# Bucket numbers of four (six) chunks packed into one word, taken apart in VectorE's registers

## The chip, the cores and the metric

The kernel runs on one core of a Trainium2 chip. The metric is the device time of one execution in microseconds (us); most executions of this kernel agree within 0.1%. The engines are TensorE (PE, with its weight loads as PEld), VectorE (DVE), ScalarE (ACT), GpSimd (POOL) and SyncE (SP). Each has a sequencer of its own that issues its instructions; in the trace the sequencer's own work (register operations, loads of registers, waits) stands under the engine's name with a q (DVEq). SBUF is the on-chip memory of 128 partitions, PSUM the memory that TensorE writes.

## The reference

Four layers over a graph with 3125 nodes of 256 features and 50000 edges: a weighted edge sum, a mixture of four experts whose gates come from a graph attention on a second graph of 32768 edges, three graph attention layers on the first graph, and a routed feed-forward layer. Cut to what the change touches:

```python
x = x + segment_sum(edge_weight[:, None] * (layernorm(x) @ W)[dst], src, 3125) + bias   # 50000 edges
def _gat_conv(x, src, dst, W, a_src, a_dst, b, n_nodes):     # once with 4 heads of 4, three times with 4 heads of 64
    h = (x @ W).reshape(n_nodes, Hh, Cc)
    e = leaky_relu(e_src[src] + e_dst[dst], 0.2)
    m = segment_max(e, dst)
    ex = exp(e - m[dst])
    denom = segment_sum(ex, dst)
    out = segment_sum(h[src] * (ex / (denom[dst] + 1e-16))[:, :, None], dst)
    return out.reshape(n_nodes, Hh * Cc) + b
```

## The kernel before, in words

The program is a row of stages, each ended by a barrier of all engines. Within a stage every engine has its own instruction list, written in the order in which it runs, and counts semaphores to wait for the others; there is no scheduler.

**The sort.** The edges of each graph are sorted by the node that they are summed into, on the chip. `place_edges` (for the edge sum) puts them into buckets of 128 nodes, `place_fine` (for the two attention graphs) into buckets of 32 nodes, 100 in all. A bucket starts at a new chunk, a column of 128 edges, so every chunk belongs to one bucket; the edge sum has 415 chunks, the attention graphs up to 360 and 504. Which bucket a chunk belongs to is found with a matrix product, and VectorE copies the numbers from PSUM into the integer tile `bucket` (L234, L359), one column a chunk, the same value in every partition. In the same stage as `place_fine` GpSimd scatters the edges of the first sort (`scatter_edges`), and VectorE goes on with `permute_edges`.

**The edge sum** (`sum_edges`). Loop over 415 chunks, unrolled. GpSimd gathers 128 rows by an indirect DMA (L651, 16 buffers), VectorE makes a 128x128 one-hot matrix (`mark`, L625), TensorE multiplies (L662, 8 banks of PSUM), VectorE adds the product to row `b` of the accumulator `acc` (`take`, L631). `b`, the bucket's number, must be in a register of VectorE's sequencer, since it enters the address. Every fourth chunk four numbers are loaded (L640). An addition waits for the product (`summed`) and for the addition before it (`taken`).

**The attention** (`attend_edges`), once 16 wide (stage from 1860 us) and three times 256 wide (from 2942, 3819 and 4693 us). Its unit is a quad of QD = 4 chunks; a loop body has U = 6 quads, a first and a last body are unrolled. For a quad q:

- GpSimd gathers four times 128 rows (L709), 6 quads ahead; before it, it waits that TensorE has used the buffer (`summed`, L707).
- VectorE prepares the scores of q + 1 (`fence`, L728), TensorE turns them (L870), VectorE reduces those of q to maxima (L757, waits for `turned`), ScalarE adds a bias (L821), VectorE carries the running maximum on (L763, L769, L774, L778) and applies the leaky slope (`leak`, L748), ScalarE takes exponentials (L831), TensorE turns back (L878), ScalarE copies (L838), TensorE forms the four sums (L886).
- VectorE adds the sums of quad q - 2 to `acc` (`add_up`, L743, four times: t = 0 to 3), each between two steps of the running maximum. The buckets' numbers come from `load_buckets` (L732), which loads four words into registers and stands after L728 and ahead of the reduction. Each addition waits for the one before it (`taken`).

After the last body the additions of the last two quads follow without other work between.

Of the kernel before, what the change touches and what calls it, by code (L numbers as in the profile page):

```python
# [10 lines left out]
NT = (N + P - 1) // P  # L11
# [6 lines left out]
HEADS = 4  # L18
QD = 4
GROUP = 24  # L20
DB = 32
STEP = 2.0 ** 50
NS = 4 * NT
LN_EPS = 1e-5
BIG = 1e30

ALU = mybir.AluOpType
# [8 lines left out]
NCS = (E + NT * (P - 1)) // P  # L36


def columns_sorted(edges):

    worst = (edges + -(-N // DB) * (P - 1)) // P
    return -(-worst // GROUP) * GROUP

# [87 lines left out]
    return 400 if edges == E else 256  # L131


def place_edges(nc, block, m, name, key_in, val_in, w_in, rec_dram, record, row, bucket):


# [21 lines left out]
    past, ps_bucket = m.work[0:NT, 0:ncol], m.psum[2][:, 0:ncol]  # L158
# [21 lines left out]
    def _(dve):  # L180
        chain = Chain(dve, steps)
# [50 lines left out]

        dve.wait_ge(counted, 1)
        chain.next(nc.vector.tensor_copy(bucket, ps_bucket))  # L234


def place_fine(nc, block, m, name, key_in, val_in, nch, record, bucket, own_hot, starts, trip_count):
# [23 lines left out]
    ps_bucket, ps_start = m.psum[2][:, 0:nch], m.psum[3][:, 0:nch]  # L261
# [21 lines left out]
    def _(dve):  # L283
        chain = Chain(dve, steps)
# [6 lines left out]
        dve.wait_ge(loaded, 32)  # L291
        nc.vector.tensor_scalar(lo_i, key, DB - 1, None, ALU.bitwise_and)
        nc.vector.tensor_scalar(valid, key, float(NT * P), None, ALU.is_lt)
        chain.next(nc.vector.tensor_scalar(place, key, 5, None, ALU.logical_shift_right))
        chain.next(nc.vector.tensor_copy(hi, place))
        for g in range(4):
            at = slice(g * NB, (g + 1) * NB)
# [24 lines left out]
            n = NB  # L322
# [31 lines left out]
        last = cend[:, NS - 1:NS]  # L354
        chain.next(nc.vector.tensor_scalar(hi[:, 0:nch // GROUP], m.iotac[:, 0:nch // GROUP], float(GROUP), last, ALU.mult, ALU.is_lt))
        chain.next(nc.vector.tensor_reduce(total[:, 0:1], hi[:, 0:nch // GROUP], AX.X, ALU.add))
        chain.next(nc.vector.tensor_scalar(trip_count, total[:, 0:1], -2.0, None, ALU.add))
        dve.wait_ge(summed, 1)
        nc.vector.tensor_copy(bucket, ps_bucket)  # L359
        chain.next(nc.vector.tensor_scalar(starts, ps_start, -BIG, None, ALU.mult))  # L360

def permute_edges(nc, block, m, name, edges, nch, record, lows, rows):

# [246 lines left out]
def sum_edges(nc, block, m, name, table, rec, index, bucket):  # L610


    hot, summed, taken, cleared = (m.sem(f"{name}_{s}") for s in ("hot", "summed", "taken", "cleared"))
    f = m.sums
    RS, PS = len(f.rows), len(f.hot)
    landed = [m.dma_sem(f"{name}_landed{s}") for s in range(RS)]
    ps = [m.psum[s][:, 0:D] for s in range(PS)]
    part = rec.rearrange("p (c k) -> p c k", k=3)

    @block.vector  # L620
    def _(dve):
        def mark(c):
            if c >= PS:
                dve.wait_ge(summed, c - PS + 1)
            nc.vector.tensor_scalar(f.hot[c % PS][:, :], m.iota[:, :], part[:, c, 0:1], part[:, c, 2:3], ALU.is_equal, ALU.mult).then_inc(hot, 1)  # L625

        def take(c, b):
            dve.wait_ge(summed, c + 1)
            if c:
                dve.wait_ge(taken, c)  # L630
            nc.vector.tensor_tensor(m.acc[:, b, 0:D], m.acc[:, b, 0:D], ps[c % PS], ALU.add).then_inc(taken, 1)  # L631

        nc.vector.memset(m.acc[:, :, :], 0.0).then_inc(cleared, 1)
        dve.wait_ge(cleared, 1)
        for c in range(PS):
            mark(c)
        for c in range(NCS):
            if c % 4 == 0:
                n = min(4, NCS - c)
                b = nc.values_load_multi_w_load_instructions(bucket[0:1, c:c + n], [mybir.EngineType.DVE], min_val=0, max_val=NT,  # L640
                                                             skip_runtime_bounds_check_because="a bucket's number counts up to 25 buckets")[1]
            take(c, b[c % 4])
            if c + PS < NCS:
                mark(c + PS)

    @block.gpsimd
    def _(pool):
        for c in range(NCS):
            if c >= RS:
                pool.wait_ge(summed, c - RS + 1)  # L650
            nc.gpsimd.indirect_dma_start(  # L651
                out=f.rows[c % RS][:, :], out_offset=None, in_=table,
                in_offset=bass.IndirectOffsetOnAxis(ap=index[:, c:c + 1], axis=0)).then_inc(landed[c % RS], 16)

    @block.tensor
    def _(pe):
        for c in range(NCS):
            pe.wait_ge(hot, c + 1)
            if c >= PS:
                pe.wait_ge(taken, c - PS + 1)  # L660
            pe.wait_ge(landed[c % RS], 16 * (c // RS + 1))
            nc.tensor.matmul(ps[c % PS], f.hot[c % PS][:, :], f.rows[c % RS][:, :], start=True, stop=True).then_inc(summed, 1)  # L662


def attend_edges(nc, block, m, name, width, table, at_dram, nch, lows, rows_in, bucket, own_hot, starts, trip_count):
# [6 lines left out]
    rw = hw + HEADS  # L672
    U = GROUP // QD
    s_ = lambda n: m.sem(f"{name}_{n}")
# [5 lines left out]
    rows = [f.rows[s][:, :, 0:rw] for s in range(U)]  # L680
# [9 lines left out]
    edges = E if nch == NCF else EG  # L690
    least, most = -(-edges // (P * GROUP)) - 2, nch // GROUP - 2

    @block.sync
    def _(sp):
        sp.dma_start(f.at[0:NS, :, :], at_dram.rearrange("q (s d) -> s q d", d=DB)).then_inc(at_in, 16)
        for h in range(HEADS):
            sp.dma_start(acc[DB * h:DB * (h + 1), :, :], table[:, h * w1:(h + 1) * w1].rearrange("(s d) c -> d s c", d=DB)).then_inc(acc_in, 16)
        sp.wait_ge(acc_in, 16 * HEADS)
# [22 lines left out]
    def _(dve):  # L721
        def fence(q, s, turn):
# [3 lines left out]
            if not isinstance(q, int) or q >= 2:  # L726
                dve.wait_ge(turned, q + (-1))
            nc.vector.tensor_tensor(f.z[s % 2], rows[s][:, :, hw:rw].unsqueeze(3).to_broadcast([P, QD, HEADS, DB]),  # L728
                                    f.pen[s % 2][:, :, :].unsqueeze(2).to_broadcast([P, QD, HEADS, DB]), ALU.subtract).then_inc(masked, 1)

        def load_buckets(q):
            return nc.values_load_multi_w_load_instructions(bucket[0:1, bass.ds(q * QD, QD)], [mybir.EngineType.DVE], min_val=0, max_val=NS - 1,  # L732
                                                            skip_runtime_bounds_check_because="a bucket's number is a sum of one-hot rows times 0 to 99")[1]

        def add_up(q, s, t, b):
            if t == 0:
# [61 lines left out]
        for k in range(2):  # L798
            q = trips * U + (2 * U - 2 + k)
            b = load_buckets(q)  # L800
            for t in range(QD):
                add_up(q, U - 2 + k, t, b[t])
# [528 lines left out]
def memory(nc, ctx):  # L1331
# [70 lines left out]
    def view(*shape):  # L1402
        n = 1
        for d in shape:
            n *= d
        v = m.work[:, at[0]:at[0] + n]
        at[0] += n
        if len(shape) == 2:
            v = v.rearrange("p (a b) -> p a b", a=shape[0])
        if len(shape) == 3:  # L1410
            v = v.rearrange("p (a b c) -> p a b c", a=shape[0], b=shape[1])
        return v
# [6 lines left out]
    f = m.flash = Memory()  # L1419
    slots = GROUP // QD  # L1420
    f.rows = [view(QD, D + 2 * HEADS) for _ in range(slots)]
# [153 lines left out]
```

## Time and profile before

| | us |
|---|---|
| median of 3 runs | 5848.58 (5844.78 to 5849.41) |
| the profiled execution | 5906.44 |
| its span | 5904.7 |
| VectorE busy | 3167.8 (54%) |
| TensorE busy, matmuls | 3100.8 (53%) |
| GpSimd busy | 2848.6 (48%) |
| ScalarE busy | 1892.7 (32%) |

The page has the busy time of each engine in 40 slices of the span, the DMA queues, and groups of instructions: line, engine, operation, names of what is written and read, shape and count, then busy time and the mean of one in ns, then the idle time of the engine just before them with what ended it. "remote" is a releaser that the trace doesn't name; "issue" is time in which the engine waited for nothing that the trace shows. Of no engine is the busy share over 54%, so the ends of waits tell more than busy times. From 1860 us on the four attention layers take up most of the time; TensorE's granted clock is 0.50 in them, 1.2 GHz.

### The profile page before, as it was taken

How to read it: one execution, taken by the hardware profiler on the slowest of the kernel's cores; microseconds unless marked ns; L12 is line 12 of the kernel's file. 1: busy time of each engine (PE TensorE's matmuls, PEld its weight loads, DVE VectorE, ACT ScalarE, POOL GpSimd, SP SyncE). 2: the span in 40 equal slices, each digit the busy share in tenths (PEclk: the TensorE clock that was granted, in tenths of full speed). 3: DMA queues.
4: the chain of work that ended last, by engine and by line, in shares of the span. 5: the costliest groups of instructions: out<-in, count | busy, mean ns of one | idle time of the engine just before them, and what ended most of it. 6: DMA issues, size and time to landing. Idle time of an engine off the chain costs nothing. (4 is left out here: it accounts for less than half of the span.)

```text
span 5904.7 us, 84687 instructions
## 1 busy us (share of the span) xinstructions
PE 3100.8 (53%) x22441; PEld 1829.3 (31%) x22441; DVE 3167.8 (54%) x8455; ACT 1892.7 (32%) x6583; POOL 2848.6 (48%) x2704
## 2 busy tenths in 40 slices
PE   0234048575735444899555555455555455555194
PEld 0111011132323222566333333333333333333163
DVE  7799999644462445111445555455555455555614
ACT  0000000000003555111155555365556256555210
POOL 2877887266643664000166665166655266655100
PEclk9678579756565555999755555655555655555597
DMA  1000000233321000000233333333333333333000
GB/s 62 25 1 4 0 1 2 70 92 91 92 61 10 8 7 6 22 7 0 64 85 80 81 80 79 74 81 80 81 81 74 81 81 80 80 80 69 16 0 24
DMA packets 200623, 297.12 MB, mean 50 GB/s; under 512 B 110599, under 2 KB 139750, under 8 KB 200454
## 3 DMA queue, kind: packets, MB, share of 16 engines
q0 software_dynamic: 108656, 245.98, 16.6%
q1 hardware_dynamic: 91830, 49.55, 3.3%
q8 instruction: 57, 0.93, 0.1%
q14 instruction: 80, 0.66, 0.0%
HBM read 272.32 MB, written 23.05 MB: 50 GB/s over the span
## 5 line engine op out<-in xcount | busy, mean ns | idle before, releaser
L709 POOL DMA_INDIRECT work<-table_att,work x1368 | 1385.5, 1013 | 1725.0 <-ACT work L807 834.5
L886 PE MATMUL psum<-work 128*32 128x65 f32 (+1 forms) x13248 | 418.2, 295 | 984.9 <-ACT work L838 974.1
L757 DVE TENSOR_REDUCE work<-psum 128x512 f32 (+1 forms) x414 | 286.0, 691 | 1164.2 <-remote 1162.0
L418 POOL DMA_INDIRECT sorted<-stage_rec,stage_row x400 | 676.7, 1692 | 177.0 <-issue 126.2
L878 PE MATMUL psum<-ident,work 128*128 128x128 f32 x1656 | 559.4, 474 | 379.2 <-ACT work L831 295.4
L886 PEld LDWEIGHTS psum<-work 128*32 128x32 f32 x13248 | 331.0, 165 | 1104.9 <-issue 1018.2
L831 ACT ACTIVATE work<-work 128x128 f32<-128x128 f32 x1656 | 529.9, 391 | 133.8 <-issue 100.3
L493 ACT ACTIVATE stats<-stats 128x25 f32<-128x25 f32 x5 | 1.1, 223 | 1697.0 <-DVE stats L483 1697.0
L651 POOL DMA_INDIRECT work<-table_sum,index x415 | 396.9, 956 | 290.2 <-SPq L1473 92.6
L838 ACT COPY work<-psum 128x512 f32<-128x512 f32 x414 | 242.7, 586 | 885.4 <-remote 829.5
L821 ACT ACTIVATE work<-psum,work 128x128 f32<-128x128 f32 x1656 | 473.7, 369 | 146.3 <-DVE work L757 97.5
L878 PEld LDWEIGHTS psum<-ident,work 128*128 128x128 f32 x1656 | 301.2, 182 | 681.9 <-ACT work L831 430.5
L662 PE MATMUL psum<-work 128*128 128x256 f32 x830 | 377.0, 584 | 251.9 <-DVE work L625 135.3
L743 DVE SCALAR_TENSOR_TENSOR acc<-acc,work,psum 128x65 f32 (+1 forms) x1656 | 445.3, 269 | 75.7 <-issue 13.3
L870 PE MATMUL psum<-ident,work 128*128 128x128 f32 x1656 | 462.0, 435 | 37.7 <-DVE work L728 26.0
L709 POOL DMA_INDIRECT work<-table_gate,work x288 | 294.7, 1023 | 310.3 <-ACT work L807 129.7
L397 PE MATMUL psum<-work 128*128 128x504 f16 (+1 forms) x1312 | 364.9, 362 | 97.7 <-DVE work L381 40.9
L814 ACT ACTIVATE work<-iota,lows 128x32 f32<-128x32 f32 x1656 | 401.8, 332 | 1.7 <-issue 1.7
L631 DVE TENSOR_TENSOR acc<-acc,psum 128x256 f32 x415 | 174.9, 421 | 320.8 <-PE psum L662 163.1
L870 PEld LDWEIGHTS psum<-ident,work 128*128 128x128 f32 x1656 | 296.3, 217 | 103.7 <-issue 71.2
L662 PEld LDWEIGHTS psum<-work 128*128 128x128 f32 x830 | 193.3, 270 | 435.7 <-DVE work L625 239.8
L728 DVE TENSOR_TENSOR work<-work 128x512 f32<-128x512 f32 x414 | 284.8, 688 | 62.5 <-DMA work<-table_att,work 29.6
(300 smaller groups left out, 4600.0 us busy)
## 6 DMA issues: line engine op xcount, KB each, us to landing
work<-table_att,work POOLq DMA_INDIRECT x1368
table_att<-acc SPq DMA_DIRECT2D x75, 132.0 KB
acc<-table_att SPq DMA_DIRECT2D x12, 812.5 KB
work<-table_sum,index POOLq DMA_INDIRECT x415
sorted<-stage_rec,stage_row POOLq DMA_INDIRECT x400
sorted<-work SPq DMA_DIRECT2D x8, 622.5 KB, 7.9
work<-sorted SPq DMA_DIRECT2D x8, 622.5 KB
work<-table_gate,work POOLq DMA_INDIRECT x288
```

The costliest lines, as they stand in the source:

```text
L397: ins = nc.tensor.matmul(ps[k], row_hot[s][:, k, :], col_hot[s], start=f == 0, stop=f == fc - 1)
L418: nc.gpsimd.indirect_dma_start(out=rec_dram[s * half + f], out_offset=bass.IndirectOffsetOnAxis(ap=m.stage_row[s][:, f:f + 1], axis=0), in ...
L651: nc.gpsimd.indirect_dma_start(out=f.rows[c % RS][:, :], out_offset=None, in_=table, in_offset=bass.IndirectOffsetOnAxis(ap=index[:, c:c + ...
L662: nc.tensor.matmul(ps[c % PS], f.hot[c % PS][:, :], f.rows[c % RS][:, :], start=True, stop=True).then_inc(summed, 1)
L709: nc.gpsimd.indirect_dma_start(out=rows[s][:, t, :], out_offset=None, in_=table[:, 0:rw], in_offset=bass.IndirectOffsetOnAxis(ap=f.index[s ...
L743: nc.vector.scalar_tensor_tensor(acc[:, b, :], acc[:, b, :], f.fac[s][:, t:t + 1], ps_s[s % 2][:, t, :], ALU.mult, ALU.add).then_inc(taken, 1)
L814: ins = nc.scalar.activation(f.pen[s % 2][:, t, :], m.iota[:, 0:DB], ACT.Square, scale=STEP, bias=lows[:, bass.ds(q * QD + t, 1)])
L821: ins = nc.scalar.activation(f.y[s % 2][:, t, :], ps_z[s % 2][:, t * P:(t + 1) * P], ACT.Identity, bias=dst[:, bass.ds(q * QD + t, 1)])
L831: nc.scalar.activation(f.pt[s % 2][:, t, :], f.y[s % 2][:, t, :], ACT.Exp, bias=f.neg[s][:, t, 1:2]).then_inc(exped, 1)
L870: ins = nc.tensor.transpose(ps_z[s % 2][:, t * P:(t + 1) * P], f.z[s % 2][:, t, :, :].rearrange("p h d -> p (h d)"), m.ident[:, :])
L878: nc.tensor.transpose(ps_p[s % 2][:, t * P:(t + 1) * P], f.pt[s % 2][:, t, :], m.ident[:, :]).then_inc(turned2, 1)
L886: ins = nc.tensor.matmul(ps_s[s % 2][DB * h:DB * (h + 1), t, :], f.p[s % 2][:, t, DB * h:DB * (h + 1)], rows[s][:, t, h * w1:(h + 1) * w1] ...
```

## The change

The numbers of several chunks are put into one integer where `bucket` is made: in `place_edges` six numbers of 5 bits (PACK0 = 6), in `place_fine` four numbers of 7 bits (QD). Column k of each group is overwritten by (column k + 1 shifted left) or (column k), from the last but one down to the first, so the first column of a group ends with all of them. That is five small operations in the first sort and three in each of the other two. In `place_fine` the copies into `starts` and `bucket` change places. `load_word` loads the one word of a group, and `unpack` makes a number of it with register operations (shift, then mask). `sum_edges` loads a word every six chunks, `load_buckets` one word a quad.

```diff
+PACK0 = 6
...
+def packs(bucket, k):
+    n = bucket.shape[1] // k
+    return bucket[:, 0:n * k].rearrange("p (q t) -> p q t", t=k)
+
+
+def load_word(dve, nc, at):
+    return nc.values_load_multi_w_load_instructions(at, [mybir.EngineType.DVE], min_val=0, max_val=2 ** 30 - 1,
+                                                    skip_runtime_bounds_check_because="bit fields of at most 30 bits")[1][0]
+
+
+def unpack(nc, dve, word, bits, t, most):
+    return nc.s_assert_within((word >> (bits * t)) & (2 ** bits - 1), 0, most, skip_runtime_bounds_check_because="packed from numbers of buckets in this range")
...
         chain.next(nc.vector.tensor_copy(bucket, ps_bucket))
+        packed = packs(bucket, PACK0)
+        for k in reversed(range(PACK0 - 1)):
+            chain.next(nc.vector.scalar_tensor_tensor(packed[:, :, k], packed[:, :, k + 1], 5, packed[:, :, k], ALU.logical_shift_left, ALU.bitwise_or))
...
         dve.wait_ge(summed, 1)
-        nc.vector.tensor_copy(bucket, ps_bucket)
-        chain.next(nc.vector.tensor_scalar(starts, ps_start, -BIG, None, ALU.mult))
+        nc.vector.tensor_scalar(starts, ps_start, -BIG, None, ALU.mult)
+        chain.next(nc.vector.tensor_copy(bucket, ps_bucket))
+        packed = packs(bucket, QD)
+        for k in reversed(range(QD - 1)):
+            chain.next(nc.vector.scalar_tensor_tensor(packed[:, :, k], packed[:, :, k + 1], 7, packed[:, :, k], ALU.logical_shift_left, ALU.bitwise_or))
...
-            if c % 4 == 0:
-                n = min(4, NCS - c)
-                b = nc.values_load_multi_w_load_instructions(bucket[0:1, c:c + n], [mybir.EngineType.DVE], min_val=0, max_val=NT,
-                                                             skip_runtime_bounds_check_because="a bucket's number counts up to 25 buckets")[1]
-            take(c, b[c % 4])
+            if c % PACK0 == 0:
+                word = load_word(dve, nc, bucket[0:1, c:c + 1])
+            take(c, unpack(nc, dve, word, 5, c % PACK0, NT))
...
         def load_buckets(q):
-            return nc.values_load_multi_w_load_instructions(bucket[0:1, bass.ds(q * QD, QD)], [mybir.EngineType.DVE], min_val=0, max_val=NS - 1,
-                                                            skip_runtime_bounds_check_because="a bucket's number is a sum of one-hot rows times 0 to 99")[1]
+            word = load_word(dve, nc, bucket[0:1, bass.ds(q * QD, 1)])
+            return [unpack(nc, dve, word, 7, t, NS - 1) for t in range(QD)]
```

The register operations of `unpack` are emitted where the number is used, behind the waits of the addition. On VectorE, in the loop of a 256 wide layer, before, from the load of a quad's numbers on (ISA is an address computation of the sequencer, REGISTER_ALU one register operation):

```order
L732 ISA
L732 TENSOR_LOAD bucket2
L757 ISA
L757 TENSOR_REDUCE work<-psum 128x4
L743 ISA
L743 SCALAR_TENSOR_TENSOR acc<-acc,work,psum 128x65
L763 ISA x2
L763 SCALAR_TENSOR_TENSOR work<-work 128x8
L742 REGISTER_ALU
L743 ISA
L743 SCALAR_TENSOR_TENSOR acc<-acc,work,psum 128x65
```

The same place of the changed kernel (its lines are 9 to 19 higher; L141 is `load_word`):

```order
L141 ISA
L141 TENSOR_LOAD bucket2
L776 ISA
L776 TENSOR_REDUCE work<-psum 128x4
L762 REGISTER_ALU
L762 ISA
L762 SCALAR_TENSOR_TENSOR acc<-acc,work,psum 128x65
L782 ISA x2
L782 SCALAR_TENSOR_TENSOR work<-work 128x8
L761 REGISTER_ALU
L762 REGISTER_ALU x2
L762 ISA
```

The order of engine instructions is the same; ahead of the first addition of a quad stands one more register operation, ahead of each of the other three stand two more.

On VectorE in the edge sum, before, from a load on:

```order
L640 TENSOR_LOAD bucket0
L631 ISA
L631 TENSOR_TENSOR acc<-acc,psum 128x256
L625 TENSOR_SCALAR work<-iota,rec 128x128
L631 ISA
```

and of the changed kernel:

```order
L141 TENSOR_LOAD bucket0
L652 REGISTER_ALU
L652 ISA
L652 TENSOR_TENSOR acc<-acc,psum 128x256
L646 TENSOR_SCALAR work<-iota,rec 128x128
L652 REGISTER_ALU x2
L652 ISA
```

Here too only register operations are added ahead of the additions, and the load comes every six chunks instead of every four. The other engines' lists are the same before and after.

## Rows read from the trace of the kernel before

**Rows 1.** The page, groups: instructions | busy, mean ns | idle before, releasers.

```profile
L709 POOL DMA_INDIRECT work<-table_att,work x1368 | 1385.5, 1013 | 1725.0 <-ACT work L807 834.5
L757 DVE TENSOR_REDUCE work<-psum 128x512 f32 (+1 forms) x414 | 286.0, 691 | 1164.2 <-remote 1162.0
```

**Rows 2.** Timeline of GpSimd, one quad: start us, us, what [idle before, releaser].

```profile
3000.73 0.95 POOL L709 DMA_INDIRECT work<-table_att,work  x1 [1.53 <-remote]
...
3005.01 0.96 POOL L709 DMA_INDIRECT work<-table_att,work  x1 [0.30 <-issue]
3007.41 0.96 POOL L709 DMA_INDIRECT work<-table_att,work  x1 [1.45 <-remote]
```

**Rows 3.** Timeline of VectorE in the same quad.

```profile
3000.17 0.69 DVE L757 TENSOR_REDUCE work<-psum 128x512 f32 x1 [3.05 <-remote]
...
3001.19 0.24 DVE L763 TENSOR_TENSOR_SCAN work<-work  x1
3001.41 0.28 DVE L743 SCALAR_TENSOR_TENSOR acc<-acc,work,psum 128x65 f32 x1
...
3002.08 0.16 DVE L774 SCALAR_TENSOR_TENSOR work<-work 128x8 f32<-128x8 f32 x1
...
3002.59 0.68 DVE L748 SCALAR_TENSOR_TENSOR work<-work 128x512 f32<-128x512 f32 x1
...
3006.85 0.69 DVE L757 TENSOR_REDUCE work<-psum 128x512 f32 x1 [2.98 <-remote]
```

**Rows 4.** Timeline of VectorE in the 16 wide layer.

```profile
2104.61 0.69 DVE L757 TENSOR_REDUCE work<-psum 128x512 f32 x1 [2.84 <-remote]
...
2111.29 0.69 DVE L757 TENSOR_REDUCE work<-psum 128x512 f32 x1 [2.85 <-remote]
```

**Rows 5.** Timeline of VectorE at the end of the first 256 wide layer.

```profile
3686.16 0.69 DVE L757 TENSOR_REDUCE work<-psum 128x512 f32 x1 [3.01 <-remote]
...
3688.88 0.68 DVE L748 SCALAR_TENSOR_TENSOR work<-work 128x512 f32<-128x512 f32 x1
...
3690.08 0.68 DVE L757 TENSOR_REDUCE work<-psum 128x512 f32 x1
...
3693.19 0.69 DVE L748 SCALAR_TENSOR_TENSOR work<-work 128x512 f32<-128x512 f32 x1 [0.61 <-ACT work L821]
...
3701.83 0.69 DVE L748 SCALAR_TENSOR_TENSOR work<-work 128x512 f32<-128x512 f32 x1 [0.45 <-ACT work L821]
...
3706.52 1.55 DVE L743 SCALAR_TENSOR_TENSOR acc<-acc,work,psum 128x65 f32 x4 [2.44 <-PE psum L886]
```

**Rows 6.** VectorE's sequencer, by line: count, duration ns min/median/max, first and last start.

```profile
L732 DVEq TENSOR_LOAD <-bucket x414: 339/344/364, 1872.3 to 5454.2; - x138
...
L640 DVEq TENSOR_LOAD <-bucket x104: 338/342/750, 1132.7 to 1726.3; - x104
...
L789 DVEq TENSOR_LOAD <-trips x4: 315/323/328, 1854.9 to 4683.6; - x4
...
L742 DVEq ALU_OP  x3: 40/40/40, 3001.2 to 3002.0; - x3
...
L743 DVEq FUSED_REGOPS  x4: 57/65/65, 3000.3 to 3002.2; - x4
```

**Rows 7.** Timeline of VectorE at the end of the edge sum.

```profile
1716.77 0.42 DVE L631 TENSOR_TENSOR acc<-acc,psum 128x256 f32 x1 [4.22 <-DMA x<-in_x_dram]
...
1717.41 0.42 DVE L631 TENSOR_TENSOR acc<-acc,psum 128x256 f32 x1
...
1728.54 0.42 DVE L631 TENSOR_TENSOR acc<-acc,psum 128x256 f32 x1 [0.21 <-DVE acc L631]
```

**Rows 8.** Timeline of GpSimd in the edge sum, two ends of pauses.

```profile
1315.94 0.95 POOL L651 DMA_INDIRECT work<-table_sum,index  x1 [3.27 <-DMA x<-in_x_dram]
...
1344.67 0.95 POOL L651 DMA_INDIRECT work<-table_sum,index  x1 [2.57 <-DMA x<-in_x_dram]
```

**Rows 9.** Timelines of GpSimd and VectorE, the last of each in the scatter's stage.

```profile
1032.12 1.10 POOL L418 DMA_INDIRECT sorted<-stage_rec,stage_row  x1 [0.30 <-issue]
...
1097.56 0.67 DVE L389 SCALAR_TENSOR_TENSOR sources<-work,psum 128x504 int32<-128x504 int32 x1
```

**Rows 10.** Timelines of VectorE and ScalarE around a pause of the gathers.

```profile
3107.53 0.69 DVE L757 TENSOR_REDUCE work<-psum 128x512 f32 x1 [2.85 <-remote]
3111.28 0.68 DVE L757 TENSOR_REDUCE work<-psum 128x512 f32 x1
3121.42 0.69 DVE L757 TENSOR_REDUCE work<-psum 128x512 f32 x1 [5.35 <-remote]
...
3112.79 0.59 ACT L838 COPY work<-psum 128x512 f32<-128x512 f32 x1 [0.54 <-PE psum L878]
```

## The prediction

> **What bounds the kernel now.** I read the page's groups first, then single quads on the timeline, then the instructions of VectorE's sequencer. A quad is four chunks of 128 sorted edges, the unit of an attention layer; a bucket number says which row of the accumulator a chunk is added to, and the change is about how VectorE gets these numbers.
>
> The page says which engine waits for which. VectorE's reduction at L757, the first step of a quad, has 1164 us of idle time before it in 414 quads, 2.8 us a quad; GpSimd's gathers at L709 have as much idle before them [rows 1]. So the attention layers, most of the time from 1860 us on, are a ring in which VectorE has air. The timeline of one quad shows what closes the ring. Reductions stand at 3000.17 and 3006.85, 6.68 us apart, with 2.98 us idle before the second [rows 3]. GpSimd issues four gathers in between, from 3000.73 to 3005.97, and is released again 1.4 us later, in the same moment as VectorE [rows 2]. The layer with 16 features, whose additions are 5 columns wide instead of 65, has the same pitch: 2104.61 to 2111.29, again 6.68 us [rows 4]. A ring bound by VectorE's chain would be shorter there. And when the gathers of a layer are over, the quads go faster, not slower: 3686.16, 3690.08 and the next ones at a pitch near 4.5 us (the additions of rows 5 stand in them). I read this so: while GpSimd issues gathers, what TensorE has finished is seen late, and a quad lasts as long as four gathers and their restart. VectorE's own work of a quad, from the reduction at 3000.17 to the end of L728 at about 3003.9, leaves 3 us of cover.
>
> In the edge sum (L631, 415 chunks) gathers bound the stage too. They come every 1.26 us with pauses: from 1315.94 to 1344.67 there are 20 of them, 1.44 us each [rows 8]. VectorE needs 0.63 us a chunk when it has a backlog [rows 7]. In the sort, VectorE itself is last: in the stage with the scatter, GpSimd's last scatter starts at 1032.12 and VectorE's last step at 1097.56 [rows 9].
>
> **The change part by part.** (1) *The load.* One word instead of four. Four words take 0.344 us in the layers and 0.342 in the edge sum; one word, the trip count, takes 0.323 [rows 6]. So a load gets 0.02 us cheaper. In the edge sum there are 70 loads instead of 104. In both places the load stands behind VectorE work already under way: from 1716.77 to 1728.54 the 18 pitches are 0.65 us on average and the first is 0.64, although every fourth chunk has a load [rows 7]. Gain on the path: 0.
>
> The Trainium skill, "Runtime: NRT & Kernel Launch", section "Instruction fetch mechanics", gives loads of sequencer registers about 200 ns for each register (it speaks of loads from HBM, these come from SBUF). By that a quad would save 0.6 us on the sequencer. The trace disagrees: four registers in 0.344 us.
>
> (2) *Taking the word apart.* A quad gets 7 register operations more: one for the first number (a mask), two for each other (shift and mask), and they stand behind the wait for the addition before and ahead of the addition itself. The recorded time of one is 0.040 us, but its place in the sequencer costs more. Between the starts of L763 at 3001.19 and L743 at 3001.41 lie 0.22 us [rows 3], with one register operation (0.040) and one address computation (0.065) [rows 6] in them. The rest, 0.115, over three steps is 0.038 each, so one register operation costs 0.078, say 0.08 us. The bounds are 0.04 (the record alone) and 0.155 (the whole gap less the 0.065). I take 0.08, since instructions of every kind there show such a gap.
>
> In a quad the operation of the first number hides under the reduction (0.69 us, while the addition waits for the engine). The other six lie between the reduction and L748, which ScalarE's exponentials wait for: 6 x 0.08 = 0.48 us a quad. In the 400 or so quads under the gathers this is covered. The exponentials and TensorE's transposes would be done at about 3005.7 instead of 3005.2 (ScalarE's copy L838 is released only with the reduction, at 3006.86); VectorE's idle 2.98 us becomes 2.5. Cost 0. If that cover were gone, it would be 414 x 0.48 = 199 us.
>
> Not covered is the end of each layer, after the last gather, four times. There the first quad's L748 at 3688.88 has no idle before it [rows 5]: +0.48. In the three that follow L748 waits for ScalarE, with 0.61 us idle at 3693.19 and 0.45 at 3701.83 [rows 5]; taking 0.45 for the two others they give 0, 0.03 and 0.03. The last four additions, 1.55 us from 3706.52, are a chain, each waiting for the one before: 7 x 0.08 = 0.56. Together 1.1 us a layer, 4.4 us for four.
>
> (3) *The edge sum.* A chunk gets 11/6 = 1.83 register operations on average, in the chain from one addition to the next (the pitch of 0.63 is 0.42 of addition and 0.21 of waiting and issue). That is +0.147 us a chunk where VectorE works off a backlog. While gathers go on this is covered, a chunk has 1.44. After the last gather, from 1716.77 to the last addition, 18 pitches are left: 18 x 0.147 = 2.6 us.
>
> (4) *Packing.* 5 + 3 + 3 small operations in the sort, of 69, 90 and 126 elements, chained. Nearest rows: 8 elements take 0.16 us (L774) and 512 take 0.68 (L748) of the same kind [rows 3], so about 0.22, 0.25 and 0.29 us, and 0.035 for the chain's wait: 1.3 + 0.85 + 0.95 = 3.1 us. VectorE is last in these stages, so all of it counts. That `starts` and `bucket` change places costs nothing: both stay, and what follows waits for both.
>
> The sum: 0 + 4.4 + 2.6 + 3.1 = 10.1 us. Against the profiled execution 5904.7 us of span become 5914.8; its own time is 5906.4, 58 us (1%) above the median of the unprofiled runs, 5848.6. I add the same 10.1 to the median: 5859 us, +0.17%. With 0.04 for a register operation the sum is 6.6 us. With 0.155 and 0.45 for a packing step it is 3.4 x 4 + 5.1 + 5.0 = 24 us. The forecast's own range is thus 5855 to 5873.
>
> **The rivals.**
> *A. A slip in the long gaps.* Slower. Every 24 quads, 14 times in all, GpSimd pauses inside a group; a quad then takes 3.7 us and the next 10.1 (the reductions stand at 3107.53, 3111.28 and 3121.42). In the first of the two VectorE is without a gap, so the 0.48 us shift ScalarE's copy from 3112.79 [rows 10] to 3113.27. If the results of TensorE are by then held back, as they are in the next gap of 5.35 us, the copy comes only at 3121.4, and TensorE's additions, on which the next gathers wait, 2.3 us later than now (copy 0.6, then the additions and their completion). It decides at a shift of L748 that reaches the point from which results are held; where that is the trace doesn't tell. Price 14 x 2.3 = 32 us: 5891. For it: the 8 gathers that follow are without a pause. Against it: the copy of before has come more than 1 us after the gathers went on, and was not held.
>
> *B. The edge sum falls into another rhythm.* Faster. A longer backlog of VectorE may let GpSimd issue more gathers between two pauses of 4 us. If 25 instead of 20 share a pause over some 250 chunks with such a rhythm, 1.26 + 4.1/25 = 1.42 instead of 1.44 gives 5 us; if one pause in three falls away, it is about 20 us: 5839. Against it: the stretches with and without long pauses have the same mean pitch, so something else seems to set it.
>
> *C. The loads were not hidden.* If 104 loads at 0.342 were on the path of the edge sum and 70 at 0.32 are, that gives 13 us, and with a quarter of 0.344 a word some 4 us in the uncovered quads: 5859 - 17 = 5842. The even pitch over the chunks with a load speaks against it [rows 7]. The page cited above would have it, and the trace did not agree.
>
> **How the numbers follow.** The forecast, 5859, has 0.62; A 0.13; B 0.10; C 0.05; 0.10 is left for what I don't see. This kernel's measurement tells a difference of about 0.2% (11.7 us) from none: the borders are 5836.9 and 5860.3. The forecast lies just inside, with about four tenths of its chance, 0.25, beyond the upper border; with A that makes slower 0.38. The rest of the forecast, B and C are no change, 0.52. The 0.10 of the unseen I give to faster, since A already takes what could go wrong on the other side. The range from 5838 to 5878 holds forecast, B and C and part of the rest, and leaves A out.
>
> **What would show it.** In the profile of the changed kernel: a bucket load near 0.32 us; additions at L762 0.16 us later against the step before; the reduction's idle time down from 2.8 us to about 2.4 a quad at an unchanged pitch of 6.7; the last chunks of the edge sum at 0.78 us; one group of packing operations each at 0.2 to 0.3 us. The forecast is wrong if the pitch of 6.7 moves, if quads after a long gap are not released where they were, or if the edge sum's last addition, 1728.5 now, moves by more than 8 us.

## The result and the profile after

The changed kernel takes 5877.7 us (median of five runs, 5875.6 to 5881.5), the kernel before in the same comparison 5848.6 (5844.8 to 5851.4). The ratio is 1.0051, with an interval from 1.0037 to 1.0066: 29 us slower. The forecast was 5859, a difference too small for this measurement to tell. The time lies just inside the upper edge of the stated range (5838 to 5878), but the kernel became slower beyond the noise, and the forecast had not said so.

The profiled execution of the changed kernel took 5875.9 us (span 5874.2). From its page, in the columns of [rows 1]:

```profile
L728 POOL DMA_INDIRECT work<-table_att,work x1368 | 1415.9, 1035 | 1668.9 <-ACT work L826 838.8
L776 DVE TENSOR_REDUCE work<-psum 128x512 f32 (+1 forms) x414 | 286.1, 691 | 987.8 <-remote 986.0
```

The reduction's idle time fell from 1164 us [rows 1] to 988; 414 x 0.46 = 190 us of register operations now stand in it. (The two profiles are no equal partners, see below; between two profiles of one chip it fell from 1124 to 982.) One quad on VectorE's timeline (start us, us, what, idle before):

```profile
3007.64 0.69 DVE L776 TENSOR_REDUCE work<-psum 128x512 f32 x1 [2.14 <-remote]
...
3008.66 0.24 DVE L782 TENSOR_TENSOR_SCAN work<-work  x1
3009.03 0.28 DVE L762 SCALAR_TENSOR_TENSOR acc<-acc,work,psum 128x65 f32 x1
...
3010.52 0.68 DVE L767 SCALAR_TENSOR_TENSOR work<-work 128x512 f32<-128x512 f32 x1
```

From scan to addition it is 0.37 us, where [rows 3] have 0.22; from reduction to the leak (L767, before L748) 2.88 instead of 2.42. The forecast had said +0.16 and +0.48; these are +0.15 and +0.46. The end of the first 256-wide layer, to be held against the last row of [rows 5]:

```profile
3693.28 0.28 DVE L762 SCALAR_TENSOR_TENSOR acc<-acc,work,psum 128x65 f32 x1 [2.01 <-PE psum L905]
...
3695.00 0.28 DVE L762 SCALAR_TENSOR_TENSOR acc<-acc,work,psum 128x65 f32 x1 [0.29 <-DVE acc L762]
```

The four additions take 2.00 us instead of 1.55. So the places that I had called exposed behave as costed. They hold only a part of the 29 us.

**Which profile to compare with.** The profiled execution of before (5906) is no partner: its quads stand 6.71 us apart in the median, those of after 6.62, and yet after is the slower kernel. The experiments explain this. They ran on three chips, and the same kernel before takes 5849 us on one (chip A below), 5901 on another (chip B) and 5250 to 5262 on a third (chip C). The profile of before that I had read looks like chip B (pitch 6.68 to 6.69 in the three variants of before profiled there; before itself was timed but not profiled on it), the runs of the result look like chip A (5849 and 5877 there too, pitch 6.60 before). All comparisons below are within one chip.

### The profile page after: what moved, and what is told of

The parts are those of the page before. It is cut to its first block and busy times, and to the rows that moved or that the text cites. A ratio compares the mean times of both kernels' runs of the same rounds, so it can differ in the third digit from the quotient of the medians.

```text
span 5874.2 us, 88322 instructions
## 1 busy us (share of the span) xinstructions
PE 3115.7 (53%) x22441; PEld 1830.1 (31%) x22441; DVE 3179.8 (54%) x8466; ACT 1890.3 (32%) x6583; POOL 2874.9 (49%) x2704
## 5 line engine op out<-in xcount | busy, mean ns | idle before, releaser
L728 POOL DMA_INDIRECT work<-table_att,work x1368 | 1415.9, 1035 | 1668.9 <-ACT work L826 838.8
L439 POOL DMA_INDIRECT sorted<-stage_rec,stage_row x400 | 663.4, 1659 | 177.2 <-issue 122.4
L681 PE MATMUL psum<-work 128*128 128x256 f32 x830 | 396.0, 605 | 236.4 <-DVE work L646 154.8
L728 POOL DMA_INDIRECT work<-table_gate,work x288 | 292.8, 1017 | 311.7 <-ACT work L826 134.9
L1287 PE MATMUL psum<-work 128*128 128x256 f32 x1200 | 298.9, 392 | 29.0 <-ACT work L1300 29.0
```

Of the source, the lines that this page charges most:

```text
L439: nc.gpsimd.indirect_dma_start(out=rec_dram[s * half + f], out_offset=bass.IndirectOffsetOnAxis(ap=m.stage_row[s][:, f:f + 1], axis=0), in ...
L728: nc.gpsimd.indirect_dma_start(out=rows[s][:, t, :], out_offset=None, in_=table[:, 0:rw], in_offset=bass.IndirectOffsetOnAxis(ap=f.index[s ...
```

## The experiments

Two accounts are held against each other. **Cover**: what the forecast says, 10 us, all of it in the packing, in the ends of the layers and in the last chunks of the edge sum. **Instructions**: each register operation costs something also where VectorE is idle.

**Chip C: the halves.** First the kernel before again, then each half of the change alone: the attention half (packing by fours and one word a quad), and the edge-sum half (packing by sixes and one word for six chunks).

> The kernel before, unchanged, for a second profile. Its profiled execution was 5906 us at a quad pitch of 6.70 us, while its median is 5849; the changed kernel was profiled at 5876 and 6.62. Theory H (the first profile showed an execution above the median): the new profile comes near 5849 with a quad pitch near 6.55 us, so that the change costs pitch in the layers. Rival (the pitch is a constant of the kernel and the difference lies elsewhere): the pitch is again 6.70 us.

> Only the attention layers' half of the change: packing in place_fine, one word a quad; the edge sum loads four words as before. My forecast's account gives +4.4 us for the layers' ends and +1.8 us for packing: 5855. If the 29 us lie in the layers (their quads or the long gaps), 5870 to 5878. If they lie in the edge sum: 5850 to 5856.

> Only the edge sum's half: packing in place_edges, one word for six chunks. My forecast's account gives +2.6 us at the stage's end and +1.3 us for packing: 5852.5. If the edge sum carries the 29 us, 5870 to 5878; if its rhythm changes for the better, below 5845.

Measured: e1_again 5263.9 beside 5262.1 for before, ratio 1.000 (0.999 to 1.001); e2_layers 0.988 (0.986 to 0.990), e3_edge 0.998 (0.997 to 0.999). All three expectations missed: this chip is 10% faster, the attention half gains 65 us on it and the edge-sum half 11. The attention groups of GpSimd in e1_again and e2_layers:

```profile
L709 POOL DMA_INDIRECT work<-table_att,work x1368 | 1392.0, 1018 | 1236.8 <-ACT work L807 821.0
```

```profile
L727 POOL DMA_INDIRECT work<-table_att,work x1368 | 1327.4, 970 | 1239.0 <-ACT work L825 823.2
```

There is no "remote" idle time of 500 us as on the other chips: gathers follow each other without pause and are the whole time of a quad. The gathers of the three 256-wide layers became shorter by 1392.0 - 1327.4 = 65 us, and these three stages by 62 us. GpSimd and VectorE of e1_again side by side show why a gather can be long:

```profile
3316.43 1.48 POOL L709 DMA_INDIRECT work<-table_att,work  x1 [0.30 <-issue]
3318.22 1.38 POOL L709 DMA_INDIRECT work<-table_att,work  x1 [0.30 <-issue]
3319.90 0.96 POOL L709 DMA_INDIRECT work<-table_att,work  x1 [0.30 <-issue]
```

```profile
3316.40 0.69 DVE L748 SCALAR_TENSOR_TENSOR work<-work 128x512 f32<-128x512 f32 x1
3318.07 0.69 DVE L728 TENSOR_TENSOR work<-work 128x512 f32<-128x512 f32 x1 [0.99 <-DMA work<-table_att,work]
```

A gather that begins at 3316.43, under the leak that ends at 3317.09, takes 1.48 us instead of 0.96. The one at 3318.22 begins under L728, which ends at 3318.76, and takes 1.38. The extra time is what is left of VectorE's step less 0.13 us (the median over the 323 gathers of e1_again that began under such a step). Both steps read two operands from SBUF. The Trainium skill, "SBUF — State Buffer", section "Who interferes with whom", states that a VectorE instruction with two SBUF inputs contends with a GpSimd instruction that reads SBUF, and the trace agrees; I call this the lock. The forecast did not weigh it.

Then the changed kernel itself (e5), the kernel before with seven register operations a quad but without packing or shorter load (e6, its edit is shown), and the attention half, packing and short load included, with fourteen operations a quad instead of seven (e8):

```diff
-            return nc.values_load_multi_w_load_instructions(...)[1]
+            words = nc.values_load_multi_w_load_instructions(...)[1]
+            return [... (w + 128 if t else w) & 127 ... for t, w in enumerate(words)]
```

> The changed kernel as it is, on the chip of the other experiments if it is the same one (before 5262 there, the attention half alone 5197, the edge-sum half alone 5251). Port theory (a gather that begins while VectorE's leak, L748 of before, still runs is lengthened by what is left of it less 0.12 us; the change moves the leak against the gathers, and the time follows from where it lands): the halves add up, 5185 +- 10. Rival (the change costs what it cost on the first chip, +29 us, whatever the chip): 5290.

> Before, with four words loaded a quad and nothing packed, but with the same seven register operations a quad in the same places as in the changed kernel. Port theory: the operations move the leak by 0.5 to 0.8 us, and that is all that counts: as the attention half, 5197 +- 10 where before is 5262, with a stretch of all gathers near 50 us instead of 128. Rival (the shorter load is what gains): 5262 +- 6. Rival (register operations cost, the load gains more): above 5268.

> The attention half with the register operations doubled, 14 a quad. Port theory: the leak starts another 0.5 us later, about 1.1 us after a gather began instead of 0.6, and so still runs when the next gather begins: about 0.4 us of stretch in most of 414 quads, 5300 to 5370 where the attention half takes 5197. Rival (later is better, or the time is hidden): 5190 to 5205.

Measured: e5_after 5191.5, ratio 0.989 (0.988 to 0.991); e6_ops 0.989 (0.987 to 0.990); e8_double 0.989 (0.988 to 0.991). The halves add up, as expected for e5, and e6 settles it for chip C: four words a quad or one is the same, and the register operations alone bring the gain. Their GpSimd groups have a mean gather of 965, 969 and 974 ns. My expectation for e8 (a leak still later collides again, 5300 and more) fell: how VectorE's steps fall against the gathers on that chip is not a matter of one fixed shift, and I have no model of it.

**Chip B: the two steps without the lock.** L728 reads its penalties, the leak the transposed features from PSUM, so that each has one SBUF operand. The leak's edit needs one more 4-wide step of VectorE a quad, and TensorE then waits for the leak before it turns the scores of a later quad; L728's edit adds no instruction:

```diff
-            nc.vector.scalar_tensor_tensor(y, y, 0.2, y, ALU.mult, ALU.max)
+            nc.vector.scalar_tensor_tensor(y, ps_z[s % 2]..., 0.2, y, ALU.mult, ALU.max)
...
+    m.flash.pen = [m.psum[6 + s][:, 0:QD * DB]... for s in range(2)]
```

> Before, with both 512-wide steps of VectorE made to read one operand from PSUM instead of two from SBUF: the leak L748 reads the transposed features there (ScalarE adds 0.8 of the node's term, the rest goes into the exponential's bias by one more 4-wide step a quad), and L728 reads the penalties there. Same result. Port theory (a gather is lengthened only by a VectorE step with two SBUF operands that already runs when it begins): every gather of the layers at 0.95 us, where before has 1.018 on average, total stretch near 0 instead of 128 us, quad pitch 5.04, and by the 66 us that 80 us less of stretch gave in the attention half, some 105 us faster than before: ratio 0.980. Rival (the lengthening is not of the operands, but of VectorE being busy): mean gather 1.0 or more, ratio 0.997 to 1.01.

> The changed kernel with the same two steps reading PSUM. Port theory: nothing is left to be gained by moving steps against the gathers, so the change no longer gains anything and costs its packing and uncovered ends, 0 to 10 us more than the kernel of the run before this, where it now gains 60. Rival (the change gains in another way on this chip): again 50 to 66 us less than the kernel of the run before this.

> Before, with the leak alone reading PSUM. Port theory: the gathers that begin under L728 are still lengthened, those under L748 not; about half of the stretch goes, mean gather of the layers 0.97 to 0.99, ratio 0.985 to 0.992. Rival (only where the steps lie counts): the extra 4-wide step moves L728 too, and the stretch is as before within 20 us.

> Before, with L728 alone reading its penalties from PSUM, nothing added and nothing moved in order. Port theory: the other half of the stretch goes, mean gather 0.97 to 0.99, ratio 0.985 to 0.992, and with the leak's run it adds up to the run with both. Rival (operands do not matter): ratio 1.00.

The four ran on a chip where before takes 5901 us, so the ratios of 0.98 to 0.99 expected for chip C could not be tried. e10: 0.9995 (0.9985 to 1.0005); e9: 1.0045 (1.003 to 1.006), 5926.1; e11: 0.9993 (0.998 to 1.000); e12: 0.9987 (0.9978 to 0.9997). The groups of e10 and e9:

```profile
L709 POOL DMA_INDIRECT work<-table_att,work x1368 | 1306.7, 955 | 1797.4 <-ACT work L810 837.9
```

```profile
L728 POOL DMA_INDIRECT work<-table_att,work x1368 | 1302.5, 952 | 1811.7 <-ACT work L829 838.1
```

The lock is gone, every gather takes 0.95 us, and with one step alone mended 0.96. So the operands are the cause of the long gathers; that part held. But the time did not move: what GpSimd saves in busy time comes back as idle time. And with the lock gone the changed kernel is still 29 us above its partner (5926.1 beside 5896.9). So the lock does not make the 29 us. (The changed kernel as it is was not run on chip B; chip A's pair without the lock, e19 and e20 below, says the same.)

**Chip A, where before takes 5849: the halves again.**

> Before, unchanged, for a profile on the chip of the three runs beside it. Ratio 1.000. On a chip where it takes some 5850 to 5900 us: stage of the edge sum 602 to 606 us, 256-wide layers 748 to 751. On one where it takes 5260: 533, 588 to 594.

> The changed kernel on the same chip. Where before takes 5850 to 5900: +29 +- 6 us, as on the first chip (ratio 1.0051) and as in the pair with free gathers (+29). Where before takes 5260: 60 us less. A chip where the cost was really the forecast's 10 us would show +10.

> The attention half alone. Where before takes 5850 to 5900: the pair with free gathers had 13 us more in its four attention stages and 2 in the sort, so +15 +- 5 is expected; rival (forecast: only the four ends of a layer, 4.4 + 1): +5; rival (all 29 are in the layers): +29. Where before takes 5260: 66 us less again.

> The edge-sum half alone. Where before takes 5850 to 5900: the pair with free gathers had 11 us more in the edge sum; VectorE, no longer able to work off its backlog between two releases (0.78 us a chunk, not 0.63), keeps TensorE and so GpSimd waiting: stage 604 becomes 612 to 616, +10 to +14 with the packing. Rival (forecast: only the drain after the last gather): +4. Where before takes 5260: the stage stays at 533 and the time within 15 us.

| kernel | us | ratio | three 256-wide layers' stages | 16-wide | edge sum |
|---|---|---|---|---|---|
| e13_before | 5849.1 | 1.000 (0.999 to 1.001) | 739.9, 738.2, 740.8 | 481.6 | 598.4 |
| e14_after | 5877.2 | 1.005 (1.004 to 1.007) | 743.0, 743.2, 743.5 | 485.0 | 607.9 |
| e15_layers | 5868.6 | 1.003 (1.002 to 1.005) | 743.5, 742.2, 744.2 | 484.8 | 601.0 |
| e16_edge | 5860.2 | 1.002 (1.001 to 1.003) | 738.6, 738.4, 739.0 | 481.7 | 611.5 |

(Stages go from one meeting of all engines to the next in the trace.) The result repeats, the halves cost 19.5 and 11.1 us and nearly add up. VectorE's reductions of e13 and e14, by line (count, ns, first and last start):

```profile
L757 DVE TENSOR_REDUCE work<-psum x414: 681/692/693, 1848.0 to 5392.3; 128x512 f32 x130, 128x4 f32<-128x512 f32 x8
```

```profile
L776 DVE TENSOR_REDUCE work<-psum x414: 678/692/693, 1862.7 to 5419.0; 128x512 f32 x130, 128x4 f32<-128x512 f32 x8
```

From first to last it is 3544.3 us before and 3556.3 after: the quads under the gathers, which should cost nothing, cost 12 us with the three ends between them. The median pitch is 6.596 in e13 and 6.624 in e14. The stages of e13 came out shorter than expected (602 to 606 and 748 to 751 were said); e14 and e15 landed in their ranges, and so did e16 but for half a microsecond of its stage. Last, on chip A too, the place of the operations (e17, its edit is shown: each number is taken out ahead of the wait), their number (e18, the attention half with 14 a quad, the same program as e8), and the pair without the lock (e19, e20):

```diff
+    reg = dve.alloc_register()
+    if t:
+        dve.reg_alu(reg, word, bits * t, ALU.logical_shift_right)
+    dve.reg_alu(reg, reg if t else word, 2 ** bits - 1, ALU.bitwise_and)
```

> The changed kernel with the same packing, the same one-word loads and the same number of register operations, but each number is taken out of the word before the wait for the addition before it: in the layers all four behind the load and ahead of the reduction, in the edge sum behind the addition before. Where before takes 5850 to 5900: theory (the place behind the wait costs): the 28 us shrink to the packing's 4 and what is seen of noise, +2 to +8; rival (the operations cost wherever they stand on VectorE's sequencer): +20 to +30. Where before takes 5260: theory (the gain there is that the leak starts later): the leak is back at its old place, so most of the 60 us gain is gone, ratio 0.997 to 1.003; rival: 0.989 again.

> The attention half with 14 register operations a quad instead of 7. Where before takes 5850 to 5900: the half with 7 cost 19 us (ratio 1.0034); if the cost goes with their number, +34 to +42 (ratio 1.006 to 1.007); if it is a step that was taken once, +19. Where before takes 5260: 0.989 as before.

> Before with both 512-wide steps reading PSUM. Where before takes 5260: the port theory as put for the first run of this kernel, gathers at 0.95 us each, ratio 0.980 (0.976 to 0.987); rival (operands do not matter) 1.00. Where before takes 5850 to 5900: ratio 0.9995 as measured.

> The changed kernel with both steps reading PSUM. Where before takes 5260: 0 to 10 us above the run before this one, since no lengthened gathers are left to be avoided; rival: 50 to 66 below it. Where before takes 5850 to 5900: 25 to 30 above it, as measured.

Measured: e17_early 5873.3, ratio 1.0041 (1.003 to 1.006); e18_double 5885.4, 1.0061 (1.004 to 1.008); e19_before_free 1.0008 (1.000 to 1.002); e20_after_free 1.0053 (1.004 to 1.007), 27.8 us above e19. Two rows of VectorE's timeline for e17, one quad apart:

```profile
3001.99 0.69 DVE L788 TENSOR_REDUCE work<-psum 128x512 f32 x1 [2.95 <-remote]
...
3008.65 0.69 DVE L788 TENSOR_REDUCE work<-psum 128x512 f32 x1 [2.68 <-remote]
```

In e17 VectorE has its idle 2.7 to 2.9 us back, since no operation stands behind the reduction any more, and the ends of the layers are back too (9.1 to 9.6 us from the last reduction to the end of the last addition, e13 9.2, e14 9.7 to 10.1). Still the median pitch is 6.63 and 24 of the 28 us remain. With 14 operations a quad it is 6.65, the 256-wide stages take 748.3, 745.8 and 747.4, and the attention half costs 36.5 instead of 19.5 us. The profiles of chip A divide this; the two middle columns are sums over the four attention stages:

| kernels | operations a quad | first to last gather, us | last gather to the stage's end, us | records over 0.6 us |
|---|---|---|---|---|
| e13, e16, e19 | as before | 2593.1 | 98.4 | 0, 0, 0 |
| e14, e15, e20 | 7 more | 2601.9 | 103.7 | 108, 115, 317 |
| e17 | 7 more, early | 2602.5 | 98.6 | 109 |
| e18 | 14 more | 2612.1 | 110.9 | 488 |

(Rows of three kernels are means. The last column counts what VectorE's sequencer did in these stages, loads, register operations and addresses.) Moving the operations ahead of the wait frees the ends of the layers and hardly more, against the +2 to +8 us that my first theory for e17 wanted; doubling them doubles what is lost under the gathers, 8.8 and 19.0 us. So that cost goes with the number of instructions and not with their place behind the wait; **cover** fell and **instructions** stands, at some 0.003 us an operation under the gathers. The shorter load and the packing were not taken apart from it on chip A, but e18 has both just as e15 has and still costs 17 us more. E20's 27.8 us, beside e19, rule out the lock for chip A. These two landed on chip A and not on C, so whether the lock is the whole of chip C's gain was not tried.

**Where an instruction costs while VectorE idles.** VectorE's sequencer at the additions of the edge sum (count, ns minimum/median/maximum), in e5_after on chip C and in e14_after on chip A:

```profile
L652 DVEq ALU_OP  x760: 40/45/64, 1128.9 to 1650.4; - x190
```

```profile
L652 DVEq ALU_OP  x760: 1/45/1385, 1132.1 to 1729.4; - x190
```

The same operation, never over 64 ns on chip C, takes up to 1385 on chip A; about a seventh of the 760 (107) take near 0.70. These are stretches in which the whole engine moves in steps. In the kernel before on chip A:

```profile
1327.09 0.42 DVE L631 TENSOR_TENSOR acc<-acc,psum 128x256 f32 x1
...
1331.29 0.42 DVE L631 TENSOR_TENSOR acc<-acc,psum 128x256 f32 x1 [3.52 <-PE psum L662]
...
1335.48 0.42 DVE L631 TENSOR_TENSOR acc<-acc,psum 128x256 f32 x1 [3.51 <-DMA x<-in_x_dram]
```

The longer gaps between additions there are 2.8, 3.5, 4.2, 4.9 and 5.6 us and little else: 4 to 8 times 0.70. They occur where gathers follow each other every 1.26 us, and I read them as VectorE's instructions coming at one per 0.70 us. A chunk has 4 of them before and about 6 after (4.26 and 6.01 records a chunk).

On the slower chips the attention layers show the same step, and only with the added operations. The load of a quad's numbers, in e13_before and in e14_after:

```profile
L732 DVEq TENSOR_LOAD <-bucket x414: 339/343/371, 1858.6 to 5397.4; - x138
```

```profile
L141 DVEq TENSOR_LOAD <-bucket x414: 4/176/722, 1872.7 to 5424.6; - x138
```

All 108 records over 0.6 us in the attention stages of e14_after begin between the third and the fourth gather of a group. The added operations push VectorE's last instructions of a quad there: in e13_before 123 of these loads begin between those two gathers, in e14_after 340. On chip C the programs of e14 and e18 (e5, e8) have no such record in these stages. This goes with the cost, but does not measure it: e20 has three times as many of these records as e14 at the same cost, and in e17 it is the register operations themselves that are long, not the load.

In the edge sum VectorE falls further behind with its longer list:

```profile
L651 POOL DMA_INDIRECT work<-table_sum,index x415: 951/956/1024, 1118.4 to 1706.8; - x139
...
L631 DVE TENSOR_TENSOR acc<-acc,psum x415: 414/422/423, 1127.2 to 1714.9; 128x256 f32 x139
```

```profile
L670 POOL DMA_INDIRECT work<-table_sum,index x415: 951/957/1022, 1123.5 to 1714.7; - x139
...
L652 DVE TENSOR_TENSOR acc<-acc,psum x415: 411/421/423, 1132.4 to 1729.6; 128x256 f32 x139
```

In e13_before the last addition starts 8.1 us after the last gather, with 9 additions to do; in e14_after 14.9 us after it, with 18. The gathers' own stretch grows from 588.4 to 591.2. Together 9.6 us, the 9.5 of the stage. The number left varies between kernels that do the same in this stage: on chip A it is 9, 16, 8 and 15 without the change (e13, e15, e18, e19) and 18, 22, 21 and 21 with it (e14, e16, e17, e20). E17 has 21 left although its backlog goes at 0.63 us a chunk again, and its stage still needs 608.9 us: the plain pace of the backlog is not what makes it longer. What makes the steps (the fetching of instructions, or semaphores and registers reached late) no run here shows. The trace of e14_after has 189 records of VectorE's sequencer over 0.6 us in this stage and only 30 packets of the instruction queues, so not every step is such a packet. The Trainium skill, "Runtime: NRT & Kernel Launch", section "Instruction fetch mechanics", calls the fetch of instructions hidden; if the steps are that fetch, it is not hidden here, but this stays open.

## Why the prediction was wrong

**The load: right.** One word takes 0.307 us (e5_after's median) against 0.343 for four, and e6_ops shows on chip C that the difference does not count. On chip A this was not tried alone.

**A register operation: right in size.** 0.46 us a quad until the leak, where 6 x 0.08 = 0.48 was said, and 0.45 for the last four additions instead of 0.56.

**The ends of the layers: right.** Last reduction to last addition takes 9.2 us before and 9.7 to 10.1 after. From the last gather to the stage's end, all four stages together, it is 5.3 us more (103.7 less 98.4); 4.4 was said.

**The packing: right.** By line, in the changed kernel's trace:

```profile
L252 DVE SCALAR_TENSOR_TENSOR bucket<-bucket x5: 282/283/284, 106.5 to 107.7; 128x69 int32<-128x69 int32 x5
...
L381 DVE SCALAR_TENSOR_TENSOR bucket<-bucket x6: 318/350/381, 361.3 to 806.6; 128x90 int32<-128x90 int32 x3, 128x126 int32<-128x126 int32 x3
```

With chaining about 3.7 us; 3.1 was said, and over the kernels of chip A the two sort stages differ by 2.3 and 0.8.

**The step that failed** is "In the 400 or so quads under the gathers this is covered ... Cost 0", with "an unchanged pitch of 6.7". The cover in time was there and was used (idle 1124 us in e13, 982 in e14), and the ring still lengthened by 0.03 us a quad: on chip A 3 x 3.8 + 3.0 = 14.4 us for the four attention stages (means of the kernels with and without the change), of which 5.3 are the ends. The term put at 0 measured some 9 us: 8.8 from the first gather to the last. I had treated idle time of VectorE as time in which added instructions are free. Why they are not stays open beyond the steps of 0.70 us shown above.

**The edge sum was mis-sized.** 2.6 us were said, 18 pitches of 0.147. Measured are +10.0 (mean of four kernels with and four without, 609.7 and 599.7). The pace of the backlog was right (0.77 us; 0.78 was said). Its length was not: I took it as fixed and counted it from 1716.77, where three gathers were still to come (the last starts at 1719.41, with 14 additions left), and on chip A it grows from 12 to 20.5 additions in the mean. That gives 6.2 of the 10 us; the other 3.8 are the gathers' own stretch, which I had taken as covered, too.

So 4.4 + 2.6 + 3.1 should have been 14.4 + 10.0 + 3.1 = 27.5 us; 28.0 are measured on chip A. **The rivals.** A (a slip in the long gaps) did not happen: those pairs of quads go from 3.75 + 10.0 to 4.10 + 9.7 us (medians of e13 and e14). B went the other way, into a longer backlog. C fell with the load. None of them was what happened, and the chance of 0.38 for slower stood mostly on the upper edge of the forecast; that 5877.7 lies in the stated range is luck, since the forecast's own bound was 5873, and that stood on dearer operations and packing, not on the terms that grew. Two of the signs that I had written as making the forecast wrong came to pass: "if the pitch of 6.7 moves", by 0.03 within one chip, a size that the 1% between the profile I read and the median had hidden; and the edge sum's last addition, which starts 14.7 us later in e14_after than in e13_before (8 was the bound).

**No version beats both kernels everywhere.** On chip C the changed kernel (0.989) and the register operations alone (0.989) are ahead. On A before is ahead of after, on B before without the lock is ahead of after without it, and only e12 (L728's penalties in PSUM) is a hair better than before, by 0.1% on chip B.

## What to carry to other kernels

An idle engine does not make added instructions free: where many gathers are issued from GpSimd, count sequencer instructions in the ring, not only time, and expect a backlog at the end of a stage to get longer with their number, also where its pace stays. VectorE's long steps can take one operand from PSUM where they run beside GpSimd's gathers: it kept the gathers short and cost at most 0.1% here. What it is worth where gathers stand back to back was not tried. Before a change is costed to some tens of us, see that profile and times come from one chip, or at least that the ring's pitch agrees with the median.

## What the runs showed of the hardware

- The same kernel takes 5849, 5901 or 5250 to 5262 us by the chip. Stages without GpSimd gathers are equal (the stage with the scatter 554.5 us on A and 554.8 on C). The edge sum takes 598 and 534 us, a 256-wide layer 740 and 588 to 594.
- A gather that begins under a VectorE step with two SBUF operands is lengthened by the rest of that step less 0.13 us (0.96 to 1.48 in the gather shown); with one operand from PSUM it stays at 0.95.
- A register operation on VectorE's sequencer is recorded at 0.045 us and takes 0.075 of its time.
- On the slower chips VectorE advances in steps of 0.70 us in stretches where gathers are issued back to back: 189 sequencer records over 0.6 us in the edge sum of e14_after, none of its register operations over 0.064 us in e5_after. In the attention stages such records appear only with the added operations (0 in e13, 108 in e14, 488 in e18) and not on the faster chip (e5, e6, e8).
- Seven register operations a quad, with packing and the short load, cost 0.3% on one chip (e15); alone they gain 1.1% on another (e6).
